# A graph layer with attention, linear attention and experts on one core: three banks for edge sums, exponents ahead of a batch's own additions, side products in halves

## The chip, the core and the metric

The kernel runs on one core of one Trainium2 chip. The core has TensorE (PE, with its weight loads PEld), VectorE (DVE), ScalarE (ACT), GpSimd (POOL) and SyncE (SP), each with its own instruction stream; they meet through semaphores. The metric is the device time of the whole program in microseconds.

## What is computed

There are 6250 nodes of 256 features and 206250 edges, sorted by destination. The output is the input plus three parts, one after the other:

```python
xn = layernorm(x)
x  = x + gat(xn, edges) + linear_attention(xn)
x  = x + expert_ffn(layernorm(x))
# gat, 8 heads of 32 columns:
h = xn @ W;  a1 = sum(h * attn_l);  a2 = sum(h * attn_r)
e = leaky_relu(a1[src] + a2[dst]);  ex = exp(e - segment_max(e)[dst])
out = segment_sum(h[src] * ex / segment_sum(ex)[dst]) + bias
# linear attention: q, k centred, squared, divided by their sums and norms
kv = k2.T @ v;  t2 = q2 @ kv / sqrt(N);  result = (v + t2) @ W_out + b_out
```

The expert part picks two of eight experts for all nodes and normalises the result.

## The kernel before

The work has three stages. The first makes, for 49 tiles of 128 nodes, the normalised features, their transpose (`xnt_d` in HBM) and the table `h_tab` of h and a1. The last stage is the expert part. Between them stands the **edge stage**, some 2600 us, which the change is about.

The edges are cut into units of 256, and a **step** adds one unit's messages to one node tile; a unit on a tile border makes two steps. `SB` = 4 steps are a **batch**, and there are 214 batches. Three batches (q = 0, 1, 2) make one turn of a loop. Each q has its own buffers `ring[q]` (gathered rows, 8 x 128), `hot[q]` and `hotT[q]` (one-hot matrices of the destinations, fp32 and bf16). For a batch b:

- POOL gathers 8 times 128 rows of `h_tab` into `ring[q]` with an indirect DMA (L613). Two gathers belong to a step, and each pair waits until the step three batches earlier has been summed (semaphore `summed`), since it overwrites that step's rows.
- SP loads the destinations for the batch three ahead after `a2c_picked`. ACT turns them into `hotT` (L698, L700, function `transposed`), copies indices (L693, `index`) and makes the exponentials into PSUM and into the ring (L706, L707, `weights`).
- PE first makes `pick(b + 1)` (L885, 8 small bf16 products), which fetches a2 and the maxima for the next batch into bank 2 and increments `a2c_picked`. Then come the four steps s0 to s3 (L920), each a sum of two fp32 products of 128x128 by 128x264 into one PSUM bank. With `MB = [3, 4]` a step waits until the step two before it has been added (`added`).
- DVE, per batch: `scale(0)` (L1330, the messages of s0 and s1 times their exponentials), the addition of the batch before's s2, `scale(1)`, the addition of its s3, `one_hots(b + 2)` (L1223), the own s0's addition (L1338), `exponents(b + 1)` (L1308 to L1313, five small operations that read bank 2), the own s1's addition. An addition adds a bank to the node tile's accumulator `acc`.

The linear attention is laid beside this as a **side** of the batches. In the first 49 turns (side "qk", one node tile a turn) PE makes q and k into bank 5 after the steps of q = 0 (L927, L929; it waits for `q2t_kept`, ACT's copy L760), ACT squares them in q = 1 (L737, L738), DVE divides them at the end of q = 2 (L1379 to L1382), ACT squares again (L741, L743), and PE adds to banks 6 and 7 and transposes q into bank 5 after the steps of q = 2 (L938, L940, L944). One turn "kv" follows, then 17 turns "mix": after each batch's steps PE makes a tile's product with `wvo` in bank 5 and with `kvw` in bank 6 (L970, L972, L974), and DVE adds them to X (L1364, L1366) in the next batch, ahead of the own s0's addition. The last turns have no side. The order on each engine is the order of the code; nothing else sorts it.

Of the kernel before, what the change touches and what calls it, by code (L numbers as in the profile page):

```python
# [23 lines left out]
ACT = mybir.ActivationFunctionType  # L24
# [3 lines left out]
P = 128  # L28
N = 6250
C = 256  # L30
H = 8
HC = C // H
KC = C // P
NT = -(-N // P)
# [9 lines left out]
MB = [3, 4]  # L44
# [3 lines left out]
R3 = 3  # L48
# [36 lines left out]
B_FIRST = KV + 1  # L85
# [24 lines left out]
def build(nc, x, src, dst, W, attn_l, attn_r, gnn_bias, W_qkv, b_qkv, W_out, b_out,  # L110
# [6 lines left out]
    with ExitStack() as ctx:  # L117
# [280 lines left out]
        def phases(eng, batch):  # L398
# [6 lines left out]
            with eng.Fori(1, A2_LAST) as i:  # L405
                three(i, "qk")
            three(A2_LAST, "qk")
            three(KV, "kv")
            three(B_FIRST, "mix", True)
# [23 lines left out]
        def _(sp):  # L433
# [45 lines left out]
            def batch(i, q, side, first):  # L479
# [4 lines left out]
                if side == "qk" and q == 0:  # L484
                    wait(sp, qk_made, i)
                    sp.dma_start(xnt_c[:].rearrange("p k n -> p (k n)"),
                                 xnt_d[bass.ds(i, 1)].rearrange("o p c -> p (o c)")).then_inc(xnt_loaded, 16)
                    if not (isinstance(i, int) and i == 0):
                        store_q2t(i - 1)
                if side == "kv" and q == 0:  # L490
                    store_q2t(NT - 1)
# [161 lines left out]
        def _(act):  # L653
# [70 lines left out]

            def batch(i, q, side, first):
                b = i * R3 + q
                last = isinstance(i, int) and i == IT
                if not last:
                    act.wait_ge(gathered[q], 16 * TB * (i + 1))
                    index(b + R3, q)  # L730
                    weights(b + 1, (q + 1) % R3)
                    transposed(b + 2, (q + 2) % R3, i + 1 if q < 1 else i + 2)
                if side == "qk":
                    if q == 1:
                        act.wait_ge(qk_made, i + 1)
                        wait(act, q2_turned, i)
                        nc.scalar.activation(q2[:], bank[5][:, 0:C], ACT.Square, accum_out=qs[:, 0:1]).then_inc(q2_squared, 1)  # L737
                        nc.scalar.activation(k2[:], bank[5][:, C:2 * C], ACT.Square, accum_out=qs[:, 1:2]).then_inc(q2_squared, 1)  # L738
                    if q == 2:
                        act.wait_ge(k2_ready, i + 1)  # L740
                        nc.scalar.activation(sq[:], q2[:], ACT.Square, accum_out=nq[:, bass.ds(i, 1)]).then_inc(k2_squared, 1)  # L741
                        act.wait_ge(k2_squared, i * 2 + 1)
                        nc.scalar.activation(sq[:], k2[:], ACT.Square).then_inc(k2_squared, 1)  # L743
                if (side == "qk" and q == 0 and not (isinstance(i, int) and i == 0)):
                    keep_q2t(i - 1)
                if side == "kv" and q == 0:
                    keep_q2t(NT - 1)
                    act.wait_ge(k2_squared, 2 * NT)
                    nc.scalar.activation(nq[:], nq[:], ACT.Sqrt).then_inc(roots, 1)
                    act.wait_ge(kx_kept, 1)  # L750
                    nc.scalar.activation(small[:, 16:16 + KC], kx[:, :, C + 1], ACT.Sqrt).then_inc(roots, 1)
                if side == "kv" and q == 1:
# [59 lines left out]
        def _(pe):  # L812
# [94 lines left out]

            def batch(i, q, side, first):
# [14 lines left out]
                if side == "qk":  # L923
                    if q == 0:
                        pe.wait_ge(xnt_loaded, (i + 1) * 16)
                        wait(pe, q2t_kept, i)
                        mm(bank[5][:], ones[0:1, :], bqk[:].rearrange("a k n -> a (k n)"), start=True, stop=False)  # L927
                        for k in range(KC):
                            ins = mm(bank[5][:], xnt_c[:, k, :], wqkv[:, k, 0:2 * C], start=False, stop=(k == KC - 1))  # L929
                        ins.then_inc(qk_made, 1)  # L930
                    if q == 2:
                        end = isinstance(i, int) and i == A2_LAST
                        begin = isinstance(i, int) and i == 0
                        n = LAST if end else P
                        pe.wait_ge(xn_made, i + 1)
                        pe.wait_ge(k2_squared, i * 2 + 2)
                        for k in range(KC):
                            mm(bank[6 + k][:, 0:C + 1], k2[0:n, k * P:(k + 1) * P], xn_c[0:n, :],  # L938
                               start=begin, stop=end, skip_group_check=True)
                            ins = mm(bank[6 + k][:, C + 1:C + 2], sq[0:n, k * P:(k + 1) * P], ones[0:n, 0:1],  # L940
                                     start=False, stop=end, skip_group_check=True)
                        ins.then_inc(kx_added, 1)
                        for k in range(KC):
                            ins = turn(bank[5][:, k * P:(k + 1) * P], q2[:, k * P:(k + 1) * P], ident[:])  # L944
                        ins.then_inc(q2_turned, 1)

                if side == "kv" and q == 1:
                    pe.wait_ge(kx_kept, 1)
                    pe.wait_ge(q2t_kept, NT)
                    for j in range(KC):  # L950
                        for k in range(KC):
                            ins = turn(bank[5][:, (j * KC + k) * P:(j * KC + k + 1) * P], kx[:, k, j * P:(j + 1) * P], ident[:])
                    ins.then_inc(kx_turned, 1)
# [598 lines left out]
```

## Time and profile before

| | us |
|---|---|
| median of three runs (3215.01 to 3229.0) | 3226.48 |
| the profiled execution | 3193.87 |
| its span | 3192.1 |
| POOL busy | 1676.3 (53%) |
| PE busy | 2246.7 (70%) |
| DVE busy | 1733.2 (54%) |
| ACT busy | 885.9 (28%) |
| mean granted TensorE clock | 0.788 of full speed |

No engine is busy all the time. The edge stage takes the span from about 100 to 2720 us; the busy shares of its 40th slices are nearly constant over it, so a few turns of the loop show what all do. The view of waits names for each idle stretch the semaphore's source ("remote" where the profile finds none), and the timeline gives instructions one by one.

### The profile page before, as it was taken

Reading aid. Unit: us, or ns where it says so; the run is one execution under the profiler, and the core shown is the slowest. Engines: PE = TensorE matmul, PEld = TensorE weight load, DVE = VectorE, ACT = ScalarE, POOL = GpSimd, SP = SyncE. Lnnn points to the kernel's source line nnn. Section 1 sums busy time; section 2 is a strip of 40 time slices with the busy share of each in tenths; the row PEclk is TensorE's granted clock in tenths of the full one; section 3 lists DMA queues with packets and bytes.
Section 4 is the critical chain, followed back from the end, with each engine's and each line's share of the span. In section 5 each row is a group of like instructions: output and inputs, shape, how many; then the busy total and the mean of one; then the engine's idle time right before and its main releaser. Section 6 shows DMA issues by size and latency. Waiting matters only on the chain.

```text
span 3192.1 us, 36971 instructions
## 1 busy us (share of the span) xinstructions
PE 2246.7 (70%) x8328; PEld 1471.7 (46%) x8329; DVE 1733.2 (54%) x3616; ACT 885.9 (28%) x1862; POOL 1676.3 (53%) x1821
## 2 busy tenths in 40 slices
PE   6566767676676666766667666777777765479997
PEld 4444444444444444444434434445444443157776
DVE  6455555555555555555555556565656555824334
ACT  3422222222222222222222223222222222334332
POOL 3566666666666666666666666666666666000000
PEclk9777777777777777777777777787877777689999
DMA  7444444444444444444444444444444444110000
GB/s 239 132 119 117 114 113 123 115 122 115 115 116 121 113 123 114 114 119 119 120 114 115 115 120 124 128 134 127 134 127 133 129 117 114 15 31 15 20 20 21
DMA packets 174887, 346.37 MB, mean 109 GB/s; under 512 B 38430, under 2 KB 91268, under 8 KB 174852
## 3 DMA queue, kind: packets, MB, share of 16 engines
q0 software_dynamic: 83296, 234.42, 27.0%
q1 hardware_dynamic: 91268, 111.28, 11.9%
q10 hardware_dynamic: 288, 0.26, 0.0%
q8 instruction: 15, 0.25, 0.0%
q14 instruction: 20, 0.16, 0.0%
HBM read 319.49 MB, written 26.33 MB: 108 GB/s over the span
## 4 chain that ended last, share of the span: by engine, by line
PE 39%; another core or an unknown queue 20%; issue 17%; DVE 15%; DVEq 4%; ACT 3%; DMA 1%; SPq 0%; POOL 0%; ACTq 0%
PE bank L920 15%; PE bank L1033 5%; DVE acc L1338 5%; PE bank L1023 4%; PE bank L929 3%; DVE zs L1308 3%; DVEq L1322 3%; PE bank L938 2%; PE bank L927 2%; PE bank L972 2%; PE bank L974 1%; PE bank L885 1%; PE bank L832 1%; ACT work L698 1%
## 5 line engine op out<-in xcount | busy, mean ns | idle before, releaser
L613 POOL DMA_INDIRECT work<-h_tab,idx x1712 | 1624.4, 949 | 983.8 <-issue 459.3
L920 PE MATMUL bank<-work 128*128 128x264 f32 x3424 | 1210.1, 503 | 722.7 <-DVE acc L1338 548.5
L920 PEld LDWEIGHTS bank<-work 128*128 128x128 f32 x3424 | 769.0, 243 | 1046.3 <-DVE acc L1338 647.0
L1338 DVE TENSOR_TENSOR acc<-bank,acc 128x264 f32 x854 | 366.5, 429 | 878.9 <-remote 579.6
L1330 DVE TENSOR_TENSOR work<-work,bank 128x1024 f32<-128x1024 f32 x428 | 520.3, 1216 | 170.5 <-issue 165.5
L706 ACT ACTIVATE bank<-zb 128x64 f32<-128x64 f32 x214 | 48.7, 228 | 1824.2 <-DVE zb L1313 1333.3
L1223 DVE TENSOR_TENSOR work<-bank,cols 128x1024 f32<-128x1024 f32 x215 | 260.9, 1214 | 0.0
L700 ACT ACTIVATE work<-work,ones 128x1024 bf16<-128x1024 bf16 x215 | 246.8, 1148 | 7.0
L698 ACT ACTIVATE work<-work,pcol 128x1024 bf16<-128x1024 bf16 x215 | 243.4, 1132 | 12.0 <-DMA work<-dst_d 12.0
L640 POOL COPY work<-acc 128x768 f32 (+2 forms) x17 | 13.6, 805 | 374.0 <-PE bank L985 296.3
L1023 PE MATMUL bank<-work 128*128 128x384 f32 (+1 forms) x544 | 177.6, 481 | 13.8 <-DMA work<-L_ffn_b 7.6
L885 PEld LDWEIGHTS bank<-a2p,work 128*128 128x128 bf16 x1712 | 95.5, 108 | 151.1 <-issue 141.5
L885 PE MATMUL bank<-a2p,work 128*128 x1712 | 102.3, 199 | 58.1 <-issue 37.7
L929 PE MATMUL bank<-wqkv,xnt_c 128*128 128x512 f32 x196 | 142.8, 869 | 0.0
L1023 PEld LDWEIGHTS bank<-work 128*128 128x128 f32 x544 | 100.7, 192 | 84.8 <-ACT work L794 8.5
L938 PE MATMUL bank<-xn_c,k 128*128 128x257 f32 (+1 forms) x196 | 109.6, 659 | 14.4 <-issue 6.0
L1308 DVE TENSOR_REDUCE zs<-bank 128x128 f32<-128x384 f32 x214 | 117.2, 548 | 1.6 <-PE bank L885 1.5
L1498 DVE TENSOR_TENSOR wqkv<-bank,acc 128x256 f32<-128x256 f32 x49 | 20.8, 425 | 160.3 <-PE bank L1033 160.3
L927 PE MATMUL bank<-bqk,ones 1*128 1x512 f32 x98 | 72.5, 828 | 40.8 <-ACT q2t_c L760 24.8
L1033 PE MATMUL bank<-work 128*128 128x256 f32 x400 | 87.8, 379 | 0.0
L929 PEld LDWEIGHTS bank<-wqkv,xnt_c 128*128 128x128 f32 x196 | 45.0, 254 | 89.1 <-issue 89.1
L1033 PE MATMUL bank<-work,cols 128*128 128x256 f32 x384 | 84.2, 379 | 0.0
(244 smaller groups left out, 1920.1 us busy)
## 6 DMA issues: line engine op xcount, KB each, us to landing
work<-dst_d SPq DMA_DIRECT2D x216, 256.0 KB
work<-h_tab,idx POOLq DMA_INDIRECT x1712
xnt_c<-xnt_d SPq DMA_DIRECT2D x66, 128.0 KB
h_tab<-acc SPq DMA_DIRECT2D x49, 132.0 KB
xnt_d<-acc SPq DMA_DIRECT2D x49, 128.0 KB
q2t_d<-q2t_c SPq DMA_DIRECT2D x49, 128.0 KB
out<-wqkv SPq DMA_DIRECT2D x16, 384.0 KB, 2.5
X<-x SPq DMA_DIRECT2D x5, 1024.0 KB, 10.0
```

What stands on the lines that cost most here:

```text
L613: nc.gpsimd.indirect_dma_start(out=ring[q][:, j, :], out_offset=None, in_=h_tab, in_offset=bass.IndirectOffsetOnAxis(ap=idx[:, q, j:j + 1] ...
L698: nc.scalar.activation(hotT[q], hotT[q], ACT.Square, bias=pcol[:]).then_inc(dst_squared, 1)
L700: nc.scalar.activation(hotT[q], hotT[q], ACT.Relu, bias=ones[:, 0:1], scale=-1.0).then_inc(hotT_ready, 1)
L885: ins = mm(bank[2][:, j * PARTS * AW:(j + 1) * PARTS * AW], hotT[q][:, j, :], a2p[:, bass.ds(ts[j // G], PARTS * AW)], start=True, stop=True)
L920: ins = mm(bank[MB[(q * SB + s) % len(MB)]][:, 0:TW], hot[q][:, s * G + g, :], ring[q][:, s * G + g, :], start=(g == 0), stop=(g == G - 1))
L929: ins = mm(bank[5][:], xnt_c[:, k, :], wqkv[:, k, 0:2 * C], start=False, stop=(k == KC - 1))
L1023: ins = mm(bank[HB[f]][:, 0:n * P], w1_sb[:, f // FC, k, (f % FC) * P:(f % FC + 1) * P], x2t[p][:, k, 0:n * P], start=(k == 0), stop=(k == ...
L1033: ins = mm(bank[4 + j][:, 0:C], hT[p][:, f, j * P:(j + 1) * P], w2_sb[:, f // FC, f % FC, :], start=(f == 0), stop=(f == TOP * FC - 1))
L1223: v.tensor_tensor(hot[q], iota_b.unsqueeze(1).to_broadcast([P, TB, P]), dstT[:, bass.ds(b * TB, TB)].unsqueeze(2).to_broadcast([P, TB, P]) ...
L1308: link(v.tensor_reduce(zs[:], pk, AX.X, ALU.add))
L1330: v.tensor_tensor(m, m, ex, ALU.mult).then_inc(msg_ready, 1)
L1338: v.tensor_tensor(a, bank[MB[(q * SB + s) % len(MB)]][:, 0:TW], a, ALU.add).then_inc(added, 1)
```

## The change

Three things are changed in the edge stage, on all five engines.

1. The sums go round three banks, `MB = [0, 3, 4]`: a step waits for the addition of the step three before it.
2. DVE makes `exponents(b + 1)` ahead of the additions of the batch's own s0 and s1, which now stand together. In a mix batch the two additions to X (L1364, L1366) come after both, at the batch's end.
3. PE's side products are cut in halves: one half stands after s1, the other after s3 (function `between`). The products for q and k move from the end of q = 0 to q = 1, ACT's first squares from q = 1 to q = 2, the sums into banks 6 and 7 from the end of q = 2 to q = 0 of the next turn, ACT's second squares with them. ACT makes these squares and its copy `keep_q2t` ahead of `weights` and `transposed` of the same batch. A turn "kv2" is added to "kv" and "mix" starts one turn later (the last turns without a side are one fewer). The product with `kvw` of a mix tile now stands after s1 of the next batch.

```diff
-MB = [3, 4]
+MB = [0, 3, 4]
-B_FIRST = KV + 1
+B_FIRST = KV + 2
```
```diff
@@ DVE, batch
+                if not last:
+                    exponents(b + 1, (q + 1) % R3, i + 1 if q < 2 else i + 2)
+                add(0)
+                add(1)
                 if side == "mix" or (side == "mix_end" and q < 2):
...
-                add(0)
-                if not last:
-                    exponents(b + 1, (q + 1) % R3, i + 1 if q < 2 else i + 2)
-                add(1)
@@ PE, batch
+                    if s % HS == HS - 1:
+                        between(i, q, side, first, s // HS)
@@ PE, new function
+            def between(i, q, side, first, half):
+                begin = isinstance(i, int) and i == 0
+                if (side == "qk" and not begin or side == "kv") and q == 0:
+                    kx_part(i - 1, half)
+                if side == "qk" and q == 1:
+                    qk_part(i, half)
...
+                t = (i - B_FIRST) * R3 + q
+                if half == 0 and ((side == "mix" and not (first and q == 0)) or (side == "mix_end" and q < 2)):
+                    mix_part(t - 1, (q - 1) % R3, None, 1)
...
@@ ACT, batch
+                if side == "qk" and not begin or side == "kv":
+                    if q == 0:
+                        squares_sq(i - 1)
+                    if q == 1:
+                        keep_q2t(i - 1)
+                if side == "qk" and q == 2:
+                    act.wait_ge(qk_made, i + 1)
...
+                if not last:
                     weights(b + 1, (q + 1) % R3)
                     transposed(b + 2, (q + 2) % R3, i + 1 if q < 1 else i + 2)
```

DVE, qk turn of the loop, q = 1, the additions and exponents of one batch (bank 1 holds a constant, bank 2 the pick), before; a row's waits are in brackets:

```order
L1223 ISA [waits summed]
L1223 TENSOR_TENSOR work<-bank1,cols 128x1024
L1338 ISA [waits added,summed]
L1338 TENSOR_TENSOR acc<-bank3,acc 128x264
L1308 TENSOR_REDUCE zs<-bank2 128x128 [waits a2c_picked,gathered2]
...
L1313 TENSOR_SCALAR zb<-zb 128x64 [waits z_own]
L1338 ISA [waits added,summed]
L1338 TENSOR_TENSOR acc<-bank4,acc 128x264
```

and after:

```order
L1254 ISA [waits summed]
L1254 TENSOR_TENSOR work<-bank1,cols 128x1024
L1339 TENSOR_REDUCE zs<-bank2 128x128 [waits a2c_picked,gathered2]
...
L1344 TENSOR_SCALAR zb<-zb 128x64 [waits z_own]
L1369 ISA [waits added,summed]
L1369 TENSOR_TENSOR acc<-bank3,acc 128x264
L1369 ISA [waits added,summed]
L1369 TENSOR_TENSOR acc<-bank4,acc 128x264
```

The first addition has gone behind the five exponent operations, which wait for PE's pick and for gathered rows, but for no sum.

PE, the same loop, from the steps of one q on; before (q = 0, the last step pair, the products for q and k, then the next batch's pick in bank 2):

```order
L920 MATMUL bank3<-work 128x264 [waits added]
L920 MATMUL bank3<-work 128x264
L95 REGISTER_ALU
L920 MATMUL bank4<-work 128x264 [waits added]
L920 MATMUL bank4<-work 128x264
L925 ISA
L927 MATMUL bank5<-bqk,ones 128x512 [waits q2t_kept,xnt_loaded]
L929 MATMUL bank5<-wqkv,xnt_c 128x512 x2
...
L885 MATMUL bank2<-a2p,work 128x48 x2
```

and after (q = 1, from s1 on):

```order
L1002 MATMUL bank4<-work 128x264 [waits added]
L1002 MATMUL bank4<-work 128x264
L920 ISA
L922 MATMUL bank5<-bqk,ones 128x512 [waits q2t_kept,xnt_loaded]
L923 MATMUL bank5<-wqkv,xnt_c 128x512
...
L1002 MATMUL bank0<-work 128x264 [waits added,msg_ready]
L1002 MATMUL bank0<-work 128x264
...
L1002 MATMUL bank3<-work 128x264 [waits added]
L1002 MATMUL bank3<-work 128x264
L923 MATMUL bank5<-wqkv,xnt_c 128x512
...
L894 MATMUL bank2<-a2p,work 128x48 x2
```

The products for q and k, with their wait for ACT's copy, now stand between two steps, and one of them behind the last.

ACT, the same loop, q = 2, after (before, the two squares into `q2` and `k2` stood at the end of q = 1, behind the exponentials and both `hotT` operations):

```order
L695 ISA [waits gathered2]
L695 COPY idx<-cols 128x8
L750 ACTIVATE q2,qs<-bank5 128x256 [waits q2_turned,qk_made]
L751 ACTIVATE k2,qs<-bank5 128x256
L708 ACTIVATE bank1<-zb 128x64 [waits u_ready]
L709 ACTIVATE work<-zb 128x8x8
L700 ACTIVATE work<-work,pcol 128x1024 [waits dst_in1]
L702 ACTIVATE work<-work,ones 128x1024 [waits dst_squared]
```

The squares, and their wait for PE's product, have moved ahead of the exponentials.

## Rows read from the trace of the kernel before

**Rows 1.** The page: span, then busy time of each engine, share, instructions.

```profile
span 3192.1 us, 36971 instructions
PE 2246.7 (70%) x8328; PEld 1471.7 (46%) x8329; DVE 1733.2 (54%) x3616; ACT 885.9 (28%) x1862; POOL 1676.3 (53%) x1821
```

**Rows 2.** The page's groups: count, busy us, mean ns, idle before and its releaser.

```profile
L613 POOL DMA_INDIRECT work<-h_tab,idx x1712 | 1624.4, 949 | 983.8 <-issue 459.3
L1338 DVE TENSOR_TENSOR acc<-bank,acc 128x264 f32 x854 | 366.5, 429 | 878.9 <-remote 579.6
```

**Rows 3.** Windows of three stretches: stretch, length, busy (count) of PE, PEld, DVE, ACT, POOL, clock, DMA.

```profile
200.00:1900.00 1700.00, 1160.53 (x4083) 724.97 (x4082) 941.26 (x1903) 465.04 (x1066) 1055.21 (x1113) 0.76 0.43 117
2020.00:2560.00 540.00, 393.60 (x1485) 263.86 (x1484) 316.75 (x615) 117.76 (x220) 332.50 (x352) 0.79 0.47 131
2600.00:2700.00 100.00, 53.21 (x199) 34.70 (x198) 52.48 (x100) 24.08 (x45) 64.67 (x69) 0.74 0.42 113
```

**Rows 4.** Waits from 200 to 1900 us: engine, line, releaser, us in total, times, longest.

```profile
POOL work L613 <- remote: 224.0, 102, 3.7
POOL work L613 <- PE bank L920: 128.1, 102, 3.4
...
DVE acc L1338 <- remote: 390.9, 108, 9.2
DVE acc L1338 <- PE bank L920: 214.8, 69, 5.8
```

**Rows 5.** Timeline, qk stretch, q = 0: start, us, engine, line, what [idle before <-releaser].

```profile
1019.55 2.03 PE L920 MATMUL bank<-work 128*128 128x264 f32 x8
...
1021.18 0.94 POOL L613 DMA_INDIRECT work<-h_tab,idx  x1 [0.30 <-issue]
1023.52 0.43 DVE L1338 TENSOR_TENSOR acc<-bank,acc 128x264 f32 x1 [2.75 <-remote]
...
1024.18 0.95 POOL L613 DMA_INDIRECT work<-h_tab,idx  x1 [2.06 <-remote]
```

**Rows 6.** Timeline of one mix batch.

```profile
2271.65 1.16 PE L920 MATMUL bank<-work 128*128 128x264 f32 x4 [1.26 <-DVE acc L1338]
...
2271.82 0.95 POOL L613 DMA_INDIRECT work<-h_tab,idx  x1 [2.43 <-PE bank L920]
...
2273.14 0.43 DVE L1338 TENSOR_TENSOR acc<-bank,acc 128x264 f32 x1
...
2274.28 1.22 DVE L1330 TENSOR_TENSOR work<-work,bank 128x1024 f32<-128x1024 f32 x1 [0.71 <-issue]
...
2277.37 2.03 PE L920 MATMUL bank<-work 128*128 128x264 f32 x8
...
2278.36 0.41 DVE L1364 TENSOR_TENSOR X<-X,bank 128x256 f32 x1
2278.91 0.48 DVE L1366 SCALAR_TENSOR_TENSOR X<-bank,nq,X 128x256 f32 x1
...
2280.59 0.95 POOL L613 DMA_INDIRECT work<-h_tab,idx  x1 [0.30 <-issue]
...
2283.30 0.43 DVE L1338 TENSOR_TENSOR acc<-bank,acc 128x264 f32 x1 [3.91 <-remote]
```

**Rows 7.** Timeline, qk stretch: PE's products for q and k behind q = 0.

```profile
1028.48 2.04 PE L927 MATMUL bank<-bqk,ones 1*128 1x512 f32 x2 [0.38 <-ACT q2t_c L760]
...
1030.45 3.78 PE L929 MATMUL bank<-wqkv,xnt_c 128*128 128x512 f32 x4
...
1036.40 0.43 DVE L1338 TENSOR_TENSOR acc<-bank,acc 128x264 f32 x1 [5.60 <-PE bank L920]
```

**Rows 8.** Groups from 200 to 1900 us: the side products' matmuls.

```profile
L929 PE MATMUL bank<-wqkv,xnt_c 128*128 128x512 f32 x184 | 133.3, 864 | 0.0
L938 PE MATMUL bank<-xn_c,k 128*128 128x257 f32 x188 | 104.8, 657 | 13.3 <-issue 6.0 <-ACT sq L743 5.4 <-ACT sq L741 1.9
```

**Rows 9.** Timeline, qk stretch, q = 1: one of ACT's four squares.

```profile
1004.16 0.37 ACT L738 ACTIVATE k<-bank 128x256 f32<-128x256 f32 x1
```

More of the change, by code:

```diff
@@ L404, in phases @@
             three(0, "qk")
-            with eng.Fori(1, A2_LAST) as i:
+            three(1, "qk")
+            with eng.Fori(2, A2_LAST) as i:
                 three(i, "qk")
@@ L487, in batch @@
                                  xnt_d[bass.ds(i, 1)].rearrange("o p c -> p (o c)")).then_inc(xnt_loaded, 16)
[L488 to L490 removed]
+                if side == "qk" and q == 1 and not (isinstance(i, int) and i == 0):
+                    store_q2t(i - 1)
+                if side == "kv" and q == 1:
                     store_q2t(NT - 1)
@@ new lines, in mix_part @@
+            def mix_part(t, q, n, k):
+                xt, q2t = (a.rearrange("p (k n) -> p k n", k=KC) for a in mix_in[q])
+                if k == 0:
+                    pe.wait_ge(mix_loaded[q], n * 32)
+                    wait(pe, mix_added, t * 2)
+                    mm(bank[5][:, 0:C], ones[0:1, :], rows[0:1, 2, :], start=True, stop=False)
+                    for k in range(KC):
+                        mm(bank[5][:, 0:C], xt[:, k, :], wvo[:, k, :], start=False, stop=(k == KC - 1))
+                else:
+                    for k in range(KC):
+                        ins = mm(bank[6][:, 0:C], q2t[:, k, :], kvw[:, k, :], start=(k == 0), stop=(k == KC - 1))
+                    ins.then_inc(mix_made, 1)
@@ L922, in batch @@
                     ins.then_inc(summed, 1)
[L923 to L953, printed above, removed]
-                if side == "kv" and q == 2:
-                    pe.wait_ge(kxt_kept, 1)
-                    kxT = wqkv[:].rearrange("p k n -> p (k n)")
-                    for k in range(KC):
-                        for j in range(KC):
-                            ins = mm(bank[6 + k][:, 0:C], kxT[:, (j * KC + k) * P:(j * KC + k + 1) * P], wvo[:, j, :],
-                                     start=(j == 0), stop=(j == KC - 1))
-                    ins.then_inc(kvw_made, 1)
@@ L1382, in batch @@
                     v.tensor_scalar(k2[:], k2[:], qs[:, 5:6], None, ALU.mult).then_inc(k2_ready, 1)
-                if side == "kv" and q == 0:
+                if side == "kv" and q == 1:
                     dve.wait_ge(kx_added, NT)
@@ L1387, in batch @@
                     dve.sem_inc(kx_kept, 1)
-                if side == "kv" and q == 1:
+                if side == "kv2" and q == 0:
                     kn = small[:, 16:16 + KC]
```

87 lines of the change are left out of this document (57 added, 30 removed).

## The prediction

> **What bounds the kernel now.** I read the busy table first [rows 1]: no engine is above 70%, so waits decide. The groups [rows 2] show the edge stage's two partners: POOL's 1712 gathers with 983.8 us idle before them, and DVE's additions L1338 with 878.9 us. Third the windows [rows 3]. A batch has 8 gathers, so its period is read from POOL's count: 1700 x 8 / 1113 = 12.22 us in the qk stretch, 540 x 8 / 352 = 12.27 us in the mix stretch, 100 x 8 / 69 = 11.59 us where no side work is left. Side work on PE of some 2 to 6 us a batch costs only 0.65 us: PE and DVE are not the bound there. Nor is POOL alone: a gather takes 0.95 us and the next follows after 0.30 us [rows 5], so 8 take 10.0 us. The other 2.2 us are POOL's long waits for sums, 224.0 + 128.1 = 352 us of the qk stretch, over its 139 batches 2.5 us each [rows 4].
>
> Fourth the timeline, for how such a wait ends. In q = 0, PE's steps s0 and s1 stand at 1019.55 to 1021.58; DVE has waited 2.75 us for s0's sum when it starts at 1023.52, 1.9 us after PE's last end; POOL's last gather had ended at 1022.12, 1.4 us before, and its next, which needs the same sum, starts at 1024.18 [rows 5]. The mix batch shows it larger [rows 6]: s0 and s1 end at 2279.40, but DVE's addition starts at 2283.30, 1.8 us after POOL's last gather ended at 2281.54. By contrast a step at 2271.65 to 2272.81, made when POOL has just begun again at 2271.82, is used by DVE at 2273.14, as soon as DVE is free. So in these rows a sum made late in POOL's run of gathers is seen only once POOL has used up its credit (the steps whose rows it may overwrite) and some 1.4 to 1.8 us have passed; POOL's first gather then starts some 0.7 us after. It is a lock: 4 steps of credit are 8 gathers, 10.0 us, and 2.2 us of handshake, 12.2 us, whatever the side. The row does not say why a finished sum is seen late; I take the pattern, not a cause.
>
> A page of the Trainium skill speaks against it: SBUF — State Buffer, section Who interferes with whom, has TensorE on ports of its own, waiting for no other engine and for no DMA. By that rule the late sums are only dependencies, which the third bank would remove; what this gives is the third rival. The same skill, Perfetto Trace Analysis, section Tensor Engine Instruction, says that the profiler estimates a matmul's end; by it the 1.9 us behind PE's last end need not be all waiting after work, which the sum doesn't rest on.
>
> **The change part by part.**
>
> *Third bank.* Of four steps in a batch, s2 no longer waits for the addition of s0. Before, one release brings s0 and s1; afterwards it can bring s0, s1 and s2, if PE isn't held otherwise. But s3 waits for s0's addition, which DVE makes after the exponents, and these wait for the pick, which is in the same late group. So the credit of one lock stays 4 steps: by itself the bank is worth nothing in a locked batch. Bounds: 0 to 2.2 us a batch.
>
> *Exponents first.* After a release DVE no longer makes the addition (0.43 us) before the five small operations, so the exponentials, `hotT` and the next pick come 0.43 us earlier. From the first addition to scale(0) it took 2274.28 - 2271.17 = 3.1 us and scale(0) takes 1.22 us [rows 6]; that stays, since both additions now follow the exponents. If nothing else holds PE, the next s0 starts 4.3 us after a release and ends a us or two later; in the mix batch it stood behind the side, and s0 and s1 ended at 2279.40, 8.2 us after [rows 6]. How long into POOL's run a sum is still seen at once, the rows bound loosely: one us in is at once, 6 us in is late [rows 6]. I put the border near 5 us, an estimate between the two: there the stretch without a side would let some s0 through, and it is the one stretch that is shorter than the lock. Each s0 that slips in gives POOL 2.5 us more run for the same 2.2 us handshake: 5 steps in 14.7 us, 11.8 us per batch. The stretch without a side, 11.59 us, is the nearest row for that.
>
> *Side products.* They cost PE nothing more (the same matmuls: 6 rows of 0.86 us for q and k, 4 of 0.66 us and small ones for the k sums [rows 8]), but their place counts. Before, 5.75 us of L927 and L929 stood ahead of the pick, and the sum was used at 1036.40 after a wait of 5.60 us [rows 7]. Afterwards q = 2 has no side at all: 11.6 us. In q = 0 and q = 1 one half, 1.3 to 1.9 us, stands ahead of the pick, the other between s1 and s2: I take the middle of 11.59 and 12.22, 11.9 us. A turn is 11.6 + 2 x 11.9 = 35.4 us instead of 36.66: 1.27 us less, times 50 turns (49 and "kv"), 63 us. Bounds: from nothing to what all batches at 10.6 us would give (half of the handshakes gone), 240 us.
>
> *ACT's squares ahead of `weights`.* Two squares of 0.37 us [rows 9], with their accumulator reads some 1 us, twice a turn, and one copy. They can start at the release, and the five small operations that ACT's exponentials need end only 1.5 us after it (2271.60, the first addition's end, to 2273.14 [rows 6]), so they are hidden; if not, ACT puts up to 1 us ahead of the exponentials twice a turn, 100 us. Queued behind them are both `hotT` operations, and PE's pick waits for those. I take 0. SP's store of q2t moves one batch later, behind the same waits, and nobody waits for it in time: 0. POOL's code is as it was.
>
> *Mix.* PE's side of one batch, between the step that ended at 2274.8 at the latest and the next pair at 2277.37 [rows 6], some 2.6 us, is split, which helps; but DVE's L1364 and L1366, 1.2 us with their gap, leave the shadow of the wait for the sum and stand between the additions and scale(0). Before, they lay at 2278.36 to 2279.39, when DVE would have waited anyway. Net 0.2 us a batch gained, 51 batches, 10 us; bounds -1 to +0.6 us a batch. The last stretch, 12 batches at 0.2 us: 2 us.
>
> Sum: 63 + 10 + 2 = 75 us. The stages before and after the edge stage are untouched. 3193.87 - 75 = 3119 us for an execution like the profiled one. That one lies 32.6 us below the median of the runs, 3226.48, which is what will be compared, so the forecast is 3226.5 - 75 = **3151 us**.
>
> **The rivals.** *One: the lock holds as it is.* Every release starts 4 steps, s0 never slips in before it is late, and all stretches stay at 12.2 us. For it: qk and mix had the same period with quite different side work [rows 3]. Against: the stretch without a side is 0.6 us better. Time: 3215 to 3240.
>
> *Two, slower: a second lock in q = 1.* PE now stands between s1 and s2 with the wait for `q2t_kept` (ACT's copy, which waits for q2's transposes) and then with half of the product, 4 rows of 0.86 us where the clock is at its lower level (1.2 GHz; the granted clock is 0.76 on average, half-way between the levels [rows 3]). Then s2 ends 0.5 + 3.4 + 1.8 = 5.7 us after the release: just where sums become late, and POOL has used up the credit of s0 and s1 after 0.7 + 5.0 = 5.7 us. If that happens, q = 1 has two handshakes. It costs 2.2 us in each of 49 turns, 108 us, less what the rest gains: about 3226 + 108 - 50 = 3285. It decides when s2 of q = 1 is seen later than 5.7 us after the release. For it: L929's long rows in exactly this place. Against: at full clock the half takes 1.7 us and s2 ends at 3.1 us.
>
> *Three: no lock, only dependencies.* If DVE's wait for s0's sum was the cause and not the sign, exponents ahead of it and three banks free the chain, and POOL's 10.0 us become the bound: at 10.0 to 10.8 us a batch, 1.4 to 2.2 us times 200 batches, 280 to 440 us less: 2790 to 2950. This is what the rule on TensorE's own ports would lead to. Against: the short fixed offset of DVE's start after POOL's last gather repeats in [rows 5] and [rows 6] (1.4 and 1.8 us), with nothing in the code that ties a sum to the gathers of another ring buffer.
>
> **How the numbers follow.** My forecast, 3080 to 3205: 0.44. The lock as it is, 3210 to 3240: 0.22. Slower by the second lock or by DVE's additions in mix, 3243 to 3340: 0.18. More gained than forecast, down to the third rival, 2790 to 3080: 0.16. The range has to leave out no more than 0.2: from 2990 (0.1 below it) to 3270 (0.1 above). 0.5% of this kernel, 16 us, is about what a measurement can tell from no change. Faster by more than that is below 3210: 0.44 + 0.16, and nearly none of rival one: 0.60. Within: 0.22. Slower: 0.18.
>
> **What would show it.** Right: POOL's count gives 11.6 to 11.9 us per batch in the qk stretch; its waits for sums fall from 352 us to some 290 us; DVE's wait moves from the first addition to the first exponent operation, which then starts right after a release; mix stays near 12.1 us. Wrong: 12.2 us everywhere (rival one); two long gaps of POOL in q = 1, with the step behind the product late (rival two); DVE never waiting more than 1 us for the pick and POOL without long gaps (rival three). The forecast fails altogether if PE's late sums turn out to hang on something other than POOL's run, such as the burst of picks and steps, since the third bank makes that burst longer.

## The result: 1.4% faster

The changed kernel takes 3176.23 us (median of four runs, 3171.85 to 3177.78) against 3224.47 us of the kernel before (four runs, 3215.01 to 3229.0). The ratio is 0.986, with a 95% interval of 0.984 to 0.988: 48 us less, where 75 were forecast. A second measurement (`a2_after`) gives 0.987 (0.985 to 0.989). No run of either shows the second, slower state.

The profiled execution after took 3176.33 us, like the median. That of before had been 31 us below its median, so between the two profiles only 17.6 us of span remain, and windows of the two understate the gain by some 30 us, 0.14 us a batch. The page, and two of its groups, against [rows 1, 2]:

```profile
span 3174.5 us, 36982 instructions
PE 2143.5 (68%) x8328; PEld 1484.5 (47%) x8329; DVE 1751.1 (55%) x3616; ACT 891.0 (28%) x1864; POOL 1673.2 (53%) x1821
...
L615 POOL DMA_INDIRECT work<-h_tab,idx x1712 | 1621.4, 947 | 972.1 <-issue 485.3
...
L1369 DVE TENSOR_TENSOR acc<-bank,acc 128x264 f32 x854 | 366.8, 429 | 558.5 <-remote 383.9
...
L1339 DVE TENSOR_REDUCE zs<-bank 128x128 f32<-128x384 f32 x214 | 117.9, 551 | 339.4 <-remote 327.3
```

DVE's idle time ahead of its additions fell from 878.9 to 558.5 us, but 339.4 us now lie ahead of its first exponent operation, where it had been 1.6 us, and POOL's idle time only went from 983.8 to 972.1 us. The wait has moved on DVE, and all of it is still there (898 us in place of 880). The windows of POOL alone say it by stretch (stretch, length, busy and count, clock, DMA share, GB/s), to be set against the counts 1113, 352 and 69 of [rows 3]:

```profile
200.00:1900.00 1700.00, 1060.36 (x1121) 0.76 0.43 118
2020.00:2560.00 540.00, 333.86 (x353) 0.79 0.48 132
2600.00:2680.00 80.00, 51.50 (x55) 0.73 0.42 115
```

With 8 gathers to a batch, the qk stretch is at 1700 x 8 / 1121 = 12.13 us a batch (before 12.22), the mix stretch at 12.24 (12.27), the stretch without a side at 11.64 (11.59). This last stretch is too short to tell: one gather more or less in 80 us is 0.2 us a batch. The waits from 200 to 1900 us, against [rows 4]:

```profile
DVE acc L1369 <- remote: 266.6, 62, 7.0
DVE zs L1339 <- remote: 222.9, 46, 11.6
...
DVE acc L1369 <- PE bank L1002: 70.3, 44, 4.0
...
POOL work L615 <- remote: 238.8, 89, 3.9
POOL work L615 <- PE bank L1002: 92.8, 77, 3.2
```

POOL waits 331.6 us for sums, where it waited 352. The timeline shows one such handshake (start, us, engine, line, what, idle before and its releaser):

```profile
1001.16 0.95 POOL L615 DMA_INDIRECT work<-h_tab,idx  x1 [0.30 <-issue]
1004.66 0.56 DVE L1339 TENSOR_REDUCE zs<-bank 128x128 f32<-128x384 f32 x1 [7.35 <-remote]
...
1005.41 0.94 POOL L615 DMA_INDIRECT work<-h_tab,idx  x1 [3.30 <-remote]
...
1006.22 0.43 DVE L1369 TENSOR_TENSOR acc<-bank,acc 128x264 f32 x1
...
1006.85 0.43 DVE L1369 TENSOR_TENSOR acc<-bank,acc 128x264 f32 x1 [0.20 <-DVE acc L1369]
```

POOL's last gather ends at 1002.11. DVE, idle for 7.35 us, can start only 2.55 us later, at 1004.66, now with the exponents; then both additions run without a wait, so their sums had been there as well. It is the pattern of the prediction, with DVE's work in the new order.

How regular this pattern is can be counted from POOL's gathers between 200 and 1900 us, taking every pause of more than 1 us as a handshake. Before, there are 139 such pauses of 2.47 us on the average, one for 8.0 gathers; but only 37 of the runs between them have exactly 8 gathers, 33 have 6 and 34 have 10. After, there are 129 pauses of 2.61 us, one for 8.7 gathers. So 8 gathers to a handshake is a mean and not a rule. The change made the runs longer and the pauses fewer, as forecast, but each pause longer too, and their sum only went from 344 to 337 us.

### The profile page after: what moved, and what is told of

It is laid out like the page before. It is cut to its first block, busy times and chain, and to the rows that moved or that the text cites. A ratio compares the mean times of both kernels' runs of the same rounds, so it can differ in the third digit from the quotient of the medians.

```text
span 3174.5 us, 36982 instructions
## 1 busy us (share of the span) xinstructions
PE 2143.5 (68%) x8328; PEld 1484.5 (47%) x8329; DVE 1751.1 (55%) x3616; ACT 891.0 (28%) x1864; POOL 1673.2 (53%) x1821
## 4 chain that ended last, share of the span: by engine, by line
PE 30%; DVE 22%; another core or an unknown queue 22%; issue 16%; DVEq 6%; ACT 2%; DMA 1%; POOL 0%; SPq 0%; ACTq 0%; POOLq 0%
PE bank L1002 13%; DVE acc L1369 7%; PE bank L1064 5%; DVE work L1254 5%; PE bank L1054 4%; DVEq L1353 4%; DVE zs L1339 2%; DVE work L1361 1%; PE bank L953 1%; PE bank L923 1%; PE bank L841 1%; PE bank L922 1%; DVEq L1369 1%; DVE zb L1342 1%
## 5 line engine op out<-in xcount | busy, mean ns | idle before, releaser
L615 POOL DMA_INDIRECT work<-h_tab,idx x1712 | 1621.4, 947 | 972.1 <-issue 485.3
L1002 PE MATMUL bank<-work 128*128 128x264 f32 x3424 | 1182.2, 497 | 782.5 <-DVE acc L1369 454.6
L1002 PEld LDWEIGHTS bank<-work 128*128 128x128 f32 x3424 | 796.0, 245 | 1055.0 <-DVE acc L1369 494.2
L1369 DVE TENSOR_TENSOR acc<-bank,acc 128x264 f32 x854 | 366.8, 429 | 558.5 <-remote 383.9
L1339 DVE TENSOR_REDUCE zs<-bank 128x128 f32<-128x384 f32 x214 | 117.9, 551 | 339.4 <-remote 327.3
L1054 PEld LDWEIGHTS bank<-work 128*128 128x128 f32 x544 | 101.0, 192 | 85.0 <-ACT work L803 8.6
L923 PE MATMUL bank<-wqkv,xnt_c 128*128 128x512 f32 x196 | 127.0, 735 | 0.0
L922 PE MATMUL bank<-bqk,ones 1*128 1x512 f32 x98 | 73.9, 842 | 32.3 <-ACT q2t_c L769 21.1
L951 PE MATMUL bank<-rows,ones 1*128 1x256 f32 x98 | 47.7, 577 | 49.0 <-DVE X L1401 39.4
L769 ACT COPY q2t_c<-bank 128x256 f32<-128x256 f32 x49 | 18.2, 372 | 220.7 <-remote 168.7
```

Of the source, the lines that this page charges most:

```text
L615: nc.gpsimd.indirect_dma_start(out=ring[q][:, j, :], out_offset=None, in_=h_tab, in_offset=bass.IndirectOffsetOnAxis(ap=idx[:, q, j:j + 1] ...
L1002: ins = mm(bank[MB[(q * SB + s) % len(MB)]][:, 0:TW], hot[q][:, s * G + g, :], ring[q][:, s * G + g, :], start=(g == 0), stop=(g == G - 1))
L1054: ins = mm(bank[HB[f]][:, 0:n * P], w1_sb[:, f // FC, k, (f % FC) * P:(f % FC + 1) * P], x2t[p][:, k, 0:n * P], start=(k == 0), stop=(k == ...
L1339: link(v.tensor_reduce(zs[:], pk, AX.X, ALU.add))
L1369: v.tensor_tensor(a, bank[MB[(q * SB + s) % len(MB)]][:, 0:TW], a, ALU.add).then_inc(added, 1)
```

## The experiments

Every ratio is to runs of the kernel before on the same chip. The chips differ, so a time in an expectation that was worked out from 3226 us is to be read as a gain. For one chip this difference is the main finding below.

### The parts, one by one

Four kernels on one chip, where the kernel before takes 3188.5 us. `p1_bank` is the kernel before with the first line of the change alone:

```diff
-MB = [3, 4]
+MB = [0, 3, 4]
```

> The kernel before with the third bank alone (MB = [0, 3, 4]), everything else as it was. Theory (the lock of POOL and PE: 4 steps of credit to one handshake, whatever the banks): within 10 us of the kernel before, 3215 to 3235. Rival (the gain is plain dependencies: s2 waits for the addition of s0): most of the 48 us that the whole change brought, 3175 to 3195.

Measured: 3179.8 us, ratio 0.997 (0.996 to 0.998).

`p2_exp` has two banks and only the order changed:

```diff
-                add(0)
                 if not last:
                     exponents(b + 1, (q + 1) % R3, i + 1 if q < 2 else i + 2)
+                add(0)
                 add(1)
```

> The kernel before with the exponents ahead of both own additions alone, two banks, sides where they were. Theory: the next s0 comes 0.43 us earlier but s2 waits for an addition that is now behind the exponents, so the gain is 0 to 20 us, 3205 to 3225. Rival (two banks and late additions collide): s2 and s3 come later than POOL's credit lasts and the kernel is slower by 0.5 us a batch or more, 3300 and above.

Measured: 3175.96 us, 0.996 (0.995 to 0.997).

`p3_halves` keeps of the change what is neither bank nor order, so the halves, the moved sides and ACT's order (the edit is against the changed kernel):

```diff
-MB = [0, 3, 4]
+MB = [3, 4]
...
+                add(0)
                 if not last:
                     exponents(b + 1, (q + 1) % R3, i + 1 if q < 2 else i + 2)
-                add(0)
                 add(1)
```

> The changed kernel with two banks and the first own addition ahead of the exponents again, so that of the change the halves and the moved side products remain. Theory (the prediction's: the place of the side sets how many s0 slip in): two thirds or more of the measured gain, 3176 to 3195. Rival (the sides are hidden behind the handshake anyway): 3215 to 3235, and the gain comes from bank and order together.

Measured: 3154.49 us, 0.990 (0.988 to 0.991), a gain of 34 us: the theory's two thirds of 48.

`p4_bank_exp` is `p1_bank` and `p2_exp` together.

> The kernel before with third bank and exponents first, sides where they were. Theory: some 10 to 20 us of gain, 3205 to 3215, since the sides still stand whole ahead of two of three picks. Rival (bank and order together are the gain, because both additions are off PE's way): 3175 to 3190.

Measured: 3153.2 us, 0.989 (0.988 to 0.991), a gain of 35 us. This is what the rival said, not the theory's 10 to 20 us.

`a2_after` is the changed kernel on another chip than these four, where the kernel before takes 3219.3 us.

> The changed kernel as it is, beside the same chip's runs of the kernel before, so that it can be set against the single parts (third bank -0.3%, exponents first -0.4%, halves -1.0%, bank and exponents -1.1%). If the parts add, ratio 0.979; if they are ways to the same gain, 0.984 to 0.987, as in the first measurement (0.986).

Measured: 3175.12 us, 0.987 (0.985 to 0.989).

| | gain |
|---|---|
| third bank | 0.3% |
| exponents first | 0.4% |
| both | 1.1% |
| halves and moved sides | 1.0% |
| everything | 1.3%, 1.4% |

Two things follow. Bank and order help each other. The waits of PE's steps for additions, from 200 to 1900 us, show how; first the kernel before, then `p1_bank`, `p2_exp` and `p4_bank_exp`:

```profile
PE bank L920 <- DVE acc L1338: 353.7, 149, 8.4
```
```profile
PE bank L920 <- DVE acc L1338: 36.5, 19, 7.5
```
```profile
PE bank L920 <- DVE acc L1338: 423.6, 150, 11.7
```
```profile
PE bank L920 <- DVE acc L1338: 238.7, 77, 10.2
```

The bank removes 317 us of PE's waits for additions and gives 9 us. PE's waits for ACT ahead of the side products took their place: they rose from 32 us to 372 us, of which `p1_bank` shows

```profile
PE bank L938 <- ACT sq L743: 238.4, 43, 6.6
PE bank L927 <- ACT q2t_c L760: 125.2, 42, 3.3
```

With two banks PE waits about once in every batch, and with the exponents first those waits grow, since s2 needs an addition that now stands behind them; the third bank halves their number, and the gain rises to 35 us. Second, the two large parts are ways to the same gain: 35 and 34 us alone, and if they added, 2.1%; measured are 1.3% and 1.4%. The whole wasn't run on the chip of its parts, so this compares ratios from different chips. In windows of the same stretch as above, `p3_halves` and `p4_bank_exp` both stand at 12.0 us a batch:

```profile
200.00:1900.00 1700.00, 1074.70 (x1134) 0.75 0.44 119
```
```profile
200.00:1900.00 1700.00, 1074.44 (x1135) 0.76 0.44 119
```

None of them comes near 11.6, and nor does the whole.

### Pauses of POOL

On the chip of `a2_after`. `t1_drain8` is the changed kernel with

```diff
@@ POOL, batch
+                    if j == 0:
+                        wait(pool, gathered[(q + 2) % R3], 16 * TB * (i + 1 if q > 0 else i))
                     if j % G == 0:
                         wait(pool, summed, SB * (b - R3) + j // G + 1)
```

> The changed kernel, but POOL waits at the start of each batch until its own last gather has landed, a pause of 1.4 to 1.5 us every 8 gathers (the last gather of a run ends on POOL 1.4 us before its data has landed). Theory (late sums come out in a pause of POOL's gathers, and the lock's 2.2 us handshake is such a pause): the deliberate pause takes the place of the handshake, 10.0 + 1.5 = 11.5 us a batch or a little more, 3040 to 3120. Rival (sums are late for another reason): the pause adds to the period, up to 1.5 us x 213 batches = 320 us more, 3400 to 3500.

`t2_drain4` adds the same wait at j == 4, for this batch's first four gathers.

> The same with the pause every 4 gathers. Theory: sums made late in POOL's run are seen at once, but two pauses a batch are 10.0 + 3.0 = 13.0 us, unless the period is set by POOL: 3330 to 3380, with POOL's waits for sums near zero. Rival (pauses add to the 12.1 us): 14 us a batch and more, above 3550.

Measured: 3356.28 us, 1.043 (1.041 to 1.045), and 3855.27 us, 1.198 (1.195 to 1.200). The first lies between theory and rival. The second lies in the rival's range (above 3550), but that range was priced with pauses of 1.5 us, and they were nearly twice as long. Waits of DVE and of POOL in `t1_drain8` from 200 to 1900 us, with one of its pauses from the timeline and the window:

```profile
DVE zs L1341 <- DMA work<-h_tab,idx: 632.3, 133, 6.7
DVE work L1363 <- issue: 94.0, 133, 1.0
DVE acc L1371 <- DVE acc L1371: 26.6, 133, 0.2
```
```profile
POOL work L617 <- DMA work<-h_tab,idx: 330.2, 112, 4.0
POOL work L617 <- issue: 282.0, 880, 2.1
POOL work L617 <- PE bank L1004: 35.0, 25, 2.7
POOL work L617 <- remote: 32.1, 12, 2.8
```
```profile
1013.92 0.94 POOL L617 DMA_INDIRECT work<-h_tab,idx  x1 [0.30 <-issue]
1017.68 0.98 POOL L617 DMA_INDIRECT work<-h_tab,idx  x1 [2.82 <-DMA work<-h_tab,idx]
```
```profile
200.00:1900.00 1700.00, 1012.18 (x1065) 0.75 0.41 112
```

With a forced pause every 8 gathers DVE no longer waits for any sum. In `a2_after`, on the same chip, it had waited for them 445 us with "remote" and 93 us for PE; now it waits for gathered rows. POOL's waits for sums fell from 322 to 67 us. The period is POOL's own: beside 7 gaps of 0.3 us a batch (the 282.0 us) POOL is idle for 408 us, 3.1 us in each of 133 batches, and 8 x 0.95 + 7 x 0.3 + 3.1 = 12.8 us (1700 x 8 / 1065 = 12.77). Added to the handshake, a pause would have made 12.1 + 2.8 = 14.9 us; it has taken its place. It only is longer than what it replaces, since it ends when the rows have landed. `t2_drain4`, with two pauses of 2.9 us, has 15.38 us by its 884 gathers in the window, though 75 of its some 220 pauses are put down to a sum of PE.

That alone doesn't prove a lock. If the period of 12.1 us had come from PE's and DVE's chain of dependencies, a POOL that takes 12.8 us would have hidden it just as well. The times at which the traces record the increments of `summed` say more. From 200 to 1900 us `t1_drain8` has 484 of them on record, and 309 came more than 0.5 us after the last step before them had ended on PE by the profile; in `a2_after` it is 320 of 436, in `t2_drain4` 1 of 405. So the pause of `t1_drain8` did not cure the late sums: they still come, 1.7 us (median) after POOL's last gather has ended, and nobody waits for them, since the rows land later still. Whether it is POOL's own rest that lets them out is open. The last packets of a gather end 1.5 us after its end on POOL (median over the pauses of `t1_drain8`), so it may as well be the gathers' traffic that a sum waits for; no run separates the two.

`t3_rows32` is the changed kernel with

```diff
+                    m = 32 if j == TB - 1 and not (isinstance(i, int) and i == 0) else P
-                        out=ring[q][:, j, :], out_offset=None, in_=h_tab,
+                        out=ring[q][0:m, j, :], out_offset=None, in_=h_tab,
```

> The changed kernel with the last gather of each batch fetching 32 rows in place of 128 (three quarters of that gather's rows are left out from the second turn on). Theory (the period is POOL's run plus a fixed handshake): the whole of what this gather gets shorter comes off each batch; if it takes 0.3 us in place of 0.95 us, 0.65 x 206 = 134 us, 3040. Rival (PE's and DVE's chain through sums, picks and exponents sets the period): no change, 3165 to 3180.

Its eighth gather leaves three quarters of its rows stale, so its sums are not those of the graph. Measured: 3161.04 us, 0.982 (0.980 to 0.984), 14 us below `a2_after`. The premise was wrong. A gather of 32 rows is hardly shorter than one of 128, 0.87 us against 0.95 us:

```profile
1506.24 0.95 POOL L616 DMA_INDIRECT work<-h_tab,idx  x1 [0.30 <-issue]
1507.50 0.87 POOL L616 DMA_INDIRECT work<-h_tab,idx  x1 [0.31 <-issue]
1510.45 0.96 POOL L616 DMA_INDIRECT work<-h_tab,idx  x1 [2.08 <-remote]
```

0.08 us x 211 batches is 17 us, about what came off, but beside `a2_after`'s own interval that tells little. With 9% fewer bytes gathered, the time moved by 0.4%.

### A chip without late sums

`t5_seven` leaves the gather out, and the waits for `gathered` count seven:

```diff
+                    if j == TB - 1 and not (isinstance(i, int) and i == 0):
+                        continue
```

> The changed kernel without the last gather of each batch from the second turn on (7 gathers in place of 8; the rows of the eighth are stale, so the sums are not those of the graph). Leaving out three quarters of that gather's rows had left its time on POOL as it was, so only this changes POOL's run: 8.75 us in place of 10.0. Lock theory: the period falls by the whole 1.25 us, to 10.9 us, 3175 - 266 = 2910. Rival (PE's and DVE's chain sets the period once the handshake is shorter): 3050 to 3150. Third (POOL's run has no part in it): 3165 to 3180.

`t6_pause` puts a shorter pause behind each batch's gathers:

```diff
+                nc.gpsimd.memset(scratch[:], 0.0).then_inc(paused, 1)
@@ next batch
+                wait(pool, paused, b)
```

> The changed kernel with a memset of 128x1152 and a wait for it behind each batch's gathers on POOL, a gap of some 1.4 us in place of 0.3 us, where the wait for landing had made 2.7 to 2.8 us and the period 12.8 us, with no late sums left. Theory (a pause of POOL lets the sums out and takes the place of the starving): if 1.4 us is enough, 10.0 + 1.2 = 11.2 to 11.6 us a batch, 2970 to 3060. Rival (it takes the landing of all gathers, some 1.5 us and more after the last one, to let them out): the pause is added to the handshake, up to 1.1 us x 214 = 235 us more, 3300 to 3410.

`n1_actlate` moves ACT's squares and copy behind the exponentials and `transposed`:

```diff
+                if not last:
+                    weights(b + 1, (q + 1) % R3)
+                    transposed(b + 2, (q + 2) % R3, i + 1 if q < 1 else i + 2)
                 if side == "qk" and not begin or side == "kv":
                     if q == 0:
                         squares_sq(i - 1)
...
-                if not last:
-                    weights(b + 1, (q + 1) % R3)
```

> The changed kernel with ACT's squares and its copy of q2 put behind weights and transposed again, in the batches to which the change moved the rest. ACT's longest waits of the changed kernel, 163 us for the copy and 112 us for q in the 1700 us, then stand behind the exponentials and not ahead of them. Theory (a late release of PE's transposes or of q and k now holds the next exponentials): faster than the changed kernel by 0.5 to 1.5%, ratio to the kernel before 0.972 to 0.982. Rival (the prediction's: they are hidden ahead of the exponentials): within 0.3% of the changed kernel, 0.984 to 0.989.

The chip that took these three gave the surprise. The kernel before, unchanged, takes **2723.72 us** there (nine runs, 2722.16 to 2728.24), 500 us less than in the first measurement. Measured: `t5_seven` 2462.51 us (ratio 0.904), `t6_pause` 3119.68 us (1.145), `n1_actlate` 2996.71 us (1.100). None of the expectations, all worked out for the other chips, holds here. The changed kernel itself was not run on this chip. `n1_actlate` was run once more, on another chip:

> The kernel n1_actlate once more. In its first runs the kernel before took 2723.7 us beside it, not 3190 to 3225 us as in all runs up to then, and its trace shows no wait of DVE or POOL for a late sum (none with remote as its source); the two kernels beside it neither. Theory (late sums belong to some chips, and where they are absent the kernel before is bound by POOL's 10.0 us a batch): where the kernel before takes 3190 us or more, this kernel's trace has the waits with remote again, some 400 to 600 us of them for DVE in the 1700 us, and the kernel takes 3150 us or more; where it takes 2724 us, 2997 us again. Rival (the order of ACT's work had removed the late sums): no remote waits even where the kernel before takes 3190 us. For ACT's order, where the kernel before takes 3190 us or more: a ratio of 0.972 to 0.982 if squares ahead of the exponentials cost something, 0.984 to 0.989 if nothing, above 1 if PE's waits for the copy and the squares, 345 us of the 1700 in the first trace, are more than that.

It met a chip where the kernel before takes 3209.4 us, and took 3283.88 us, ratio 1.023 (1.021 to 1.025). The same kernel on two chips, windows of a part of the mix stretch, which has no work of ACT's side in it; `n1_actlate`, then `n2_actlate` (busy and count of PE, PEld, DVE, ACT, POOL, clock, DMA share, GB/s):

```profile
2020.00:2400.00 380.00, 307.79 (x1282) 221.54 (x1283) 277.12 (x536) 101.71 (x190) 287.43 (x305) 0.83 0.57 160
```
```profile
2020.00:2400.00 380.00, 262.06 (x1008) 189.90 (x1007) 222.80 (x435) 91.52 (x172) 236.61 (x251) 0.77 0.47 129
```

305 gathers are 9.97 us a batch, which is POOL's 8 x 1.25 us and nothing else; 251 are 12.11 us, the period of the kernels with late sums. POOL's waits in the same window, in the same order of kernels:

```profile
POOL work L615 <- issue: 80.7, 265, 0.3
...
POOL work L615 <- PE bank L1002: 11.6, 38, 0.3
```
```profile
POOL work L615 <- issue: 77.2, 212, 3.5
...
POOL work L615 <- PE bank L1002: 33.5, 24, 2.6
POOL work L615 <- remote: 32.5, 14, 2.9
```

The longest wait of POOL for a sum is 0.3 us on the one chip and 2.9 us on the other, with the same code and inputs. The recorded increments agree: none of 567 came late on the first of these chips (median 0.014 us after PE's profiled end), 128 of 502 did on the second. PE's busy time is 8.1 and 8.4 us a batch, and a gather takes 0.94 us on both, so slower engines don't explain the 2.1 us between them. The handshake of 2.2 us is thus no dependency of the kernel. It is what the late sums cost, and these occur in some measurements and not in others: the kernel before shows 3188 to 3225 us in four of five measurements and 2724 us in one. 500 us over 214 batches is 2.3 us a batch, the whole handshake. (The kernel before has no trace from that chip; this is read from its time.) DVE's waits for late sums in `n2_actlate`, from 200 to 1900 us, are back too, and its time is above the 3150 us that was expected with them, though the waits are only 97 us and not 400 to 600; in that stretch PE now waits mostly for ACT, as shown below:

```profile
DVE zs L1339 <- remote: 55.1, 18, 3.8
DVE acc L1369 <- remote: 41.8, 23, 3.9
```

What delays the sums on the other chips isn't shown; the granted clock is lower there (0.77 against 0.83 above), but PE is idle for 19% and 31% of the two windows, so that may be a result of the waits as well as a part of their cause. Nor is it shown that the chip as such makes the difference: only one measurement was taken on it, and its traces differ in one more way. They hold nearly all increments by DMAs (21915 of 22064 in the 1700 us of `n1_actlate`), those of the other chips a fraction (5591 of 20416 in `n2_actlate`). Whether whatever loses these records also delays the sums is open.

`t5_seven` then says what the change is worth where sums come in time:

```profile
200.00:1700.00 1500.00, 1179.68 (x5117) 826.07 (x5115) 1186.26 (x2347) 555.59 (x1240) 1135.17 (x1198) 0.87 0.56 151
```

1500 x 7 / 1198 = 8.76 us a batch, which is 7 x 1.25: even here PE and DVE of the changed code keep up with POOL. With the eighth gather 211 x 1.25 = 264 us come back, 2726 us: as much as the kernel before takes on that chip, 2724. That is an estimate, since the changed kernel wasn't run there. Both kernels would then be bound by POOL, and the change worth nothing there. The test of the lock that `t5_seven` was meant for (2910 us) didn't take place, since nothing is locked here.

`t6_pause`'s question, whether a shorter pause lets sums out, stayed open for the same reason. On this chip a pause is only a cost: the memset takes 1.08 us, and POOL then waits for its end (116.0 us in 122 waits, 0.95 us each). The two make a gap of 2.0 us, where I had allowed 1.4 us and where 0.3 us stand without them, and the kernel is 394 us above the estimate for the changed one, 1.8 us a batch.

```profile
L621 POOL MEMSET scratch<- 128x1152 f32 x143 | 154.0, 1077 | 0.0
```
```profile
POOL work L618 <- POOL scratch L621: 116.0, 122, 1.0
```

For ACT's order both runs say the same: it must not be put back. The theory had it faster and the rival the same; it is slower, as `n2_actlate`'s expectation allowed. On chips with late sums the changed kernel stands at 0.987 and this one at 1.023, 3.7% more. In the qk stretch its waits of PE are, in `n1_actlate` and in `n2_actlate`:

```profile
PE bank L935 <- ACT sq L732: 197.2, 48, 4.5
PE bank L1002 <- DVE work L1361: 163.7, 49, 3.5
PE bank L922 <- ACT q2t_c L769: 147.9, 47, 3.5
```
```profile
PE bank L935 <- ACT sq L732: 297.5, 44, 8.0
```

The first halves of the products for the k sums (L935, in q = 0) and for q and k (L922, in q = 1) stand between s1 and s2, so PE waits there for ACT, and s2 and s3 wait behind it, and POOL behind those (451.5 us of waits for sums in `n2_actlate`, where it had been 331.6). This is the second rival of the prediction, PE held between s1 and s2, brought about by another order on ACT. It decided even without late sums: `n1_actlate` is 10% slower than the kernel before on the chip where that one takes 2724 us.

## Why the prediction was right, and where it was too high

**The sign** held, and the result, 3176 us, lies 25 us above the forecast of 3151 us and inside its band of 3080 to 3205. **The mechanism** held in part. That POOL's 2.2 us beyond its 10.0 us of gathers [rows 3 to 6] belong to sums that are seen late, and not to the work of PE and DVE, is borne out: on the chip without late sums the kernel before takes 2.3 us a batch less. That the handshake comes every 4 steps and always costs 2.2 us is not: the runs between pauses mostly have 6 to 12 gathers, and longer runs ended in longer pauses (8.0 gathers and 2.47 us before, 8.7 and 2.61 us after). The third rival (2790 to 2950 if the late sums were only dependencies) was rightly held unlikely, but for a reason that goes further than I knew: where sums aren't late, the old order is enough for 10.0 us. By the Trainium skill, SBUF — State Buffer, section Who interferes with whom, TensorE waits for no other engine; the chip at 2724 us agrees with that. On the others it is the increment that is late; whether the matmul was held too can't be told from ends that the profile models, and no run names what delays it.

**Some of it was luck.** Bank and order together, which the sum put at nothing, bring 35 us alone; the sides, put at 63 us, bring 34 us. The total came within the band because the one stood in for the other.

**The third bank** was put at nothing by itself, with bounds of 0 to 2.2 us a batch. It gives 9 us, 0.04 us a batch. That step held for the bank alone; with the exponents first it is worth 23 us (13 to 35 us).

**Exponents first** was given no sum of its own. Alone it is 13 us, with the bank 35 us. The step had seen that s3 waits for s0's addition behind the exponents; it hadn't weighed that with two banks s2 does so too, in each batch, so that the two parts belong together.

**The side products** were the term that was too large: 63 us. Halves and moved sides alone brought 34 us, and on top of bank and order the rest of the way from 1.1% to 1.3 or 1.4%, 8 to 12 us, hardly more than the intervals, and from different chips. The failed step is the one that set q = 2 to 11.6 us and q = 0 and q = 1 to the middle of 11.6 and 12.2. The windows show 12.13 us a batch in the profiled execution after, and 12.0 us in the best of the other kernels. Steps did slip in, but the forecast had every handshake stay at 2.2 us, and they grew. The border "near 5 us into POOL's run" was an estimate from two loose rows, and too much hung on it. The 11.6 us came from 69 gathers in a stretch without a side; as a price for q = 2 alone, which has neighbours with sides, it was too good. The upper bound of this term, 240 us, was also mis-worked: with half of the 2.2 us handshakes gone a batch takes 11.1 us and not 10.6, which makes some 165 us. It did not enter the forecast.

**ACT's squares** were put at 0 with a bound of 100 us. That no better place is behind the exponentials is shown (3.7% more). That they cost nothing where they are is not: in the trace after, ACT waits ahead of the exponentials for late transposes, up to 13.7 us at a time, and for q and k:

```profile
ACT q2t_c L769 <- remote: 163.3, 25, 13.7
ACT q L750 <- remote: 112.2, 17, 8.3
```

What that costs, and whether it is part of the missing 27 us, stays open.

**Mix** was put at 10 us and 0.2 us a batch. The windows give 12.27 before and 12.24 after, some 2 us in all, from counts that differ by one gather. Together with the last stretch, 2 us forecast and none seen, this is the smaller part of the error.

**What would show it** was half right. DVE's wait did move in part to the first exponent operation (222.9 us, the longest 11.6 us). POOL's waits for sums fell to 332 us, not to 290, and its count gives 12.13, not 11.6 to 11.9 us. The choice of the median of before, and not its fast profiled execution, as the base was right: the medians differ by 48 us, the profiled executions by 17.5.

## What to carry to other kernels

When a wait's length repeats whatever the work beside it, look at when the semaphore was incremented and not only at when the waiting engine went on. A forced pause of the other engine shows whether the wait is replaced or added, but a plain dependency can hide behind a long pause as well as a lock can. Price a reordering by the stretch where it acts, not by the best stretch of the kernel, and expect two ways of hiding the same wait not to add. Before tuning against a wait that no line of the code explains, time the kernel on several chips: here the whole wait, 15% of the time, was absent in the measurement on one of them, where by the estimate above the change gains nothing.

## What was not expected of the hardware

- The kernel before took 2723.7 us on one chip and 3188 to 3224 us in the other measurements. The runs of each measurement agree within 0.5%; only the profiled execution of the kernel before, 3193.87 us, lies outside, 0.7% below the lowest run beside it.
- In `a2_after` 320 of the 436 increments of `summed` on record from 200 to 1900 us came more than 0.5 us after PE's profiled end, in `n1_actlate` none of 567, with 0.014 us as the median.
- From the end of POOL's last gather to the start of a gather that waits for its rows it took 2.82 us in the row shown and 2.95 us on the average (330.2 us in 112 waits, `t1_drain8`); from the same point to the first use of a late sum 1.4 to 2.6 us in the three places shown.
- A gather of 32 rows takes 0.87 us on POOL, one of 128 rows 0.95 us; the gap to the next is 0.30 us for both.
